# Three late loads moved behind later stores, and two rounding steps moved from the vector to the scalar engine, in the closing stage of a feed-forward kernel

## The reference, cut to what matters

```python
w = weights[conditions]                            # 128 matrices of 64x64
c = jnp.einsum('bct,bcd->bdt', x, w)               # x: 128 x 64 x 512, fp32
h = jnp.einsum('bsd,hd->bsh', c, ternarize(W1, 0.05)) + b1   # 512 -> 2048
h = jax.nn.gelu(h, approximate=False)
y = jnp.einsum('bsh,dh->bsd', h, ternarize(W2, 0.05)) + b2   # 2048 -> 512
scale = jnp.max(jnp.abs(y)) / 7.0 + 1e-08          # one scale over ALL of y
q = jnp.clip(jnp.round(y / scale), -7.0, 7.0) * scale
return x + q
```

## Time and profile before

| what | value |
|---|---|
| median of 3 runs | 1003.65 us (1003.36 to 1004.45) |
| the profiled execution, its own time | 1004.09 us |
| span of its records, first instruction to last | 1002.2 us |
| mean granted clock of the tensor engine | 0.974 |
| tensor engine busy | 925.8 us (92%) |
| vector engine, scalar engine busy | 644.5 us (64%), 547.3 us (55%) |
| main memory read, written | 60.89 MB, 16.78 MB |
| GB/s in the last four of 40 slices of 25 us | 168, 313, 385, 390 |

### The profile page before, as it was taken

The page is one execution under the profiler, slowest core; times in us unless marked ns, Lnnn a source line. Parts: engine busy times, 40 slices in busy tenths (PEclk is TensorE's granted clock), DMA queues, the critical chain, the costliest instruction groups (busy, mean ns, idle before and its releaser), DMA issues.

```text
span 1002.2 us, 14662 instructions
## 1 busy us (share of the span) xinstructions
PE 925.8 (92%) x5136; PEld 440.1 (44%) x5136; DVE 644.5 (64%) x1024; ACT 547.3 (55%) x690; POOL 144.8 (14%) x187
## 2 busy tenths in 40 slices
PE   2999999999999999999999999999999999999700
PEld 2544444444444444444444444444444444444300
DVE  7998576665656666656657666665666665633493
ACT  6886728274473827365372827446382836536190
POOL 4400030301203030200203030110303030000000
PEclk9999999999999999999999999999999999999955
DMA  9501103012212102111210301121210301204899
GB/s 341 154 2 43 43 14 82 10 42 44 50 42 51 43 10 59 32 45 42 52 42 25 69 10 42 46 48 42 52 42 10 69 23 44 84 0 168 313 385 390
DMA packets 24318, 77.86 MB, mean 78 GB/s; under 512 B 3952, under 2 KB 4080, under 8 KB 23792
## 3 DMA queue, kind: packets, MB, share of 16 engines
q1 hardware_dynamic: 20032, 73.41, 24.6%
q0 software_dynamic: 3840, 3.94, 1.4%
q10 hardware_dynamic: 432, 0.34, 0.1%
HBM read 60.89 MB, written 16.78 MB: 77 GB/s over the span
## 4 chain that ended last, share of the span: by engine, by line
PE 80%; issue 9%; DVE 5%; ACT 2%; DMA 1%; POOL 0%; SPq 0%; DVEq 0%; POOLq 0%; ACTq 0%
PE ps L433 39%; PE ps L443 37%; PE ps L413 3%; PE ps L494 3%; ACT y L706 1%; DMA y<-in_L_ffn_W 1%; DVE st L907 1%; DVE wts L866 1%; DVE wts L1046 1%; DVE wts L756 1%; DVE y L1046 0%; SPq L275 0%; DVE yc L772 0%; POOL odd L354 0%; DVE wts L911 0%
## 5 line engine op out<-in xcount | busy, mean ns | idle before, releaser
L433 PE MATMUL ps<-yc,wts 128*128 128x512 f16 x2048 | 444.9, 379 | 0.0
L443 PE MATMUL ps<-wts 128*128 128x512 f16 x1792 | 391.4, 379 | 0.0
L433 PEld LDWEIGHTS ps<-yc,wts 128*128 128x128 f16 x2048 | 200.4, 98 | 241.5 <-ACT g L610 0.4
L756 DVE SCALAR_TENSOR_TENSOR wts<-g,st,wts 128x512 f16<-128x512 f32 x256 | 186.4, 749 | 140.2 <-ACT wts L615 138.5
L610 ACT ACTIVATE g<-ps,b1t,st 128x512 f32<-128x512 f32 x256 | 197.9, 774 | 123.3 <-PE ps L433 106.7
L443 PEld LDWEIGHTS ps<-wts 128*128 128x128 f16 x1792 | 173.4, 98 | 204.8
L615 ACT ACTIVATE wts<-g,st 128x512 f16<-128x512 f32 x256 | 181.0, 713 | 0.0
L597 ACT ACTIVATE xs<-yx,st 128x2048 f16<-128x2048 f32 x28 | 56.1, 2002 | 136.8 <-DVE st L790 136.8
L365 POOL PARTITION_ALL_REDUCE st<-st x46 | 21.8, 473 | 663.3 <-DVE st L725 416.1
L348 POOL DMA_INDIRECT odd<-in_L_cond_weights,odd x112 | 110.1, 983 | 41.5 <-issue 30.0
L761 DVE SCALAR_TENSOR_TENSOR y<-ps,st,b2b 128x512 f32 (+1 forms) x56 | 41.6, 747 | 79.8 <-PE ps L443 79.7
(11 more groups left out here) (131 smaller groups left out, 366.8 us busy)
## 6 DMA issues: line engine op xcount, KB each, us to landing
yx<-in_x SPq DMA_DIRECT2D x56, 512.0 KB, 6.3
wts<-in_x SPq DMA_DIRECT2D x10, 512.0 KB, 5.4
out<-wts SPq DMA_DIRECT2D x10, 512.0 KB, 14.0
y<-in_L_ffn_W SPq DMA_DIRECT2D x8, 512.0 KB, 8.8
wts<-in_x SPq DMA_DIRECT2D x4, 1024.0 KB, 5.0
y<-in_L_ffn_W SPq DMA_DIRECT2D x4, 1024.0 KB, 20.5
y<-in_x SPq DMA_DIRECT2D x3, 1024.0 KB, 9.4
out<-wts SPq DMA_DIRECT2D x3, 1024.0 KB, 13.0
```

The lines of the kernel that those rows point to most:

```text
L433: last = nc.tensor.matmul(psH[:, j % HB, :], T1T[:, j // HC, k, j % HC * P:(j % HC + 1) * P], csp[:, a, k, :], start=(k == 0 and a == 0), ...
L443: last = nc.tensor.matmul(psY[:, r % 2, :], hsp[:, a, j, r * P:(r + 1) * P], T2T[:, j, :], start=(j == 0 and a == 0), stop=(j == HT - 1 an ...
L756: nc.vector.scalar_tensor_tensor(out=hsp[:, 1, j, :], in0=g[:, j % HB, :], scalar=s_h, in1=hsp[:, 0, j, :], op0=ALU.mult, op1=ALU.subtract ...
```

## The change

Two edits. First, `load_tail` of 13, 14 and 15 is issued behind the stores of blocks 3, 4 and 5, not 0, 1 and 2; the places that they load into stay the same. Second, `BY_VECTOR` holds piece 0 alone, so the scalar engine rounds pieces 1 and 3 too.

```diff
-        BY_VECTOR = (0, 1, 3)
+        BY_VECTOR = (0,)
...
+            WITH = 3
             stores = 0
             for i, (b, m, n) in enumerate(PIECES):
                 sp.wait_ge(o_made, i + 1)
                 for rows, source, cols in transfers(b, m, n):
                     sp.dma_start(rows_of(out_v, rows, cols), source).then_inc(o_stored, 16)
                     stores += 1
-                if i == LAST_OF[b] and b < NB - XS:
-                    load_tail(b + XS)
+                if i == LAST_OF[b] and WITH <= b < WITH + NB - XS:
+                    load_tail(b - WITH + XS)
```

## The result

| | before | after |
|---|---|---|
| median, 22 runs each | 1004.04 us (1003.36 to 1005.91) | 1005.48 us (1005.12 to 1006.7) |
| span of the profiled execution | 1002.2 us | 1003.8 us |

The ratio after to before is 1.0013, 95% interval 1.0008 to 1.0019: the changed kernel is slower by 0.8 to 1.9 us. That is clear of noise and less than the 0.2% that were called no change. On the scale of the three runs that the forecast started from (1003.65 us) the ratio gives 1004.95, inside 1003.1 to 1005.4; the bare median of the larger set, whose before is itself 0.4 higher, lies 0.1 above that range.

What follows compares the result with a forecast made beforehand. The prediction took bytes in the DMA queue, at 420 GB/s, to set the end. Its terms, -1.92, +2.3, +0.1 and 0 for roundings, gave +0.5 us; it expected 1004.1 us, range 1003.1 to 1005.4.

Steps and rivals of the forecast that it cites:

- slow stretch at 953.4 to 958 goes: Closing stage, around L13's old turn: DMA engines busy at 245 GB/s lose 1.92 us, which the change was to save.
- dry queue ahead of s2: Closing stage: after block 1's stores the DMA queue runs empty until block 2's store starts, costing 2.3 us (2.0 to 2.7).
- L13 at its new turn: Closing stage, at 962.9 to 963.6 us: L13, 3.4 to 4.1 us ahead of its turn, costs 0.1 us (0 to 1.92).
- roundings: Closing stage: moving pieces 1 and 3 to the scalar engine makes block 2 on 0.3 us later, worth 0.
- a dip of 1 us or more at L13's turn: Sign against the forecast, at about 963 us: it would mean the queue's depth isn't what hides a read.
- the read is dear wherever it stands: Rival at L13's turn: switching from stores to the first load costs 1.92 us anywhere; +2.7, 1006.4 us; chance 0.11.
- the rival beside it: Rival ahead of block 2's store: the gap is smaller, 1.4 us lost; sum -0.5, 1003.2 us; chance 0.2.
- the rival in which it never does: Rival: block 2's store finds the DMA engines still at work, so 1.92 us are saved; 1001.7 us; chance 0.04.
- their work on the same memory: Rival: ACT and DVE memory work makes 953.4 to 958 us slow, whatever is queued; -0.1 to +0.3, 1003.8 us; chance 0.1.

Runs made afterwards that it cites:

- e2: Kernel before with only the rounding edit (the vector engine rounds piece 0 alone), late loads still behind blocks 0 to 2; 1003.84 against 1003.60 us.
- e4: Changed kernel with the late loads behind the stores of blocks 6 to 8; 1005.41 us, +1.81 against the kernel before.
- f4: Changed kernel with the three late loads issued from the scalar engine, in another queue than the stores; 1003.81 us, +0.27 against the kernel before.
- e3: Changed kernel with the three late loads in reverse order, 15, 14, 13; 1005.24 us, +1.64 against the kernel before.
- f2: Changed kernel with a quarter of L13 behind block 0 and the rest behind block 3; 1004.37 us, +0.83 against the kernel before.
- g1: Kernel before with late loads issued ahead of the stores of blocks 0 to 2, in the stores' pieces; 1003.60 against 1003.58 us.
- f1: Changed kernel without the three late loads, so 3.1 MB less are moved; 996.94 us in four runs, -6.6 against the kernel before.
- f3: Changed kernel with L13 behind block 0, L14 and L15 behind blocks 6 and 7; 1004.90 us, +1.36 against the kernel before.
- g3: Changed kernel with the late loads behind blocks 1 to 3; 1003.87 us, +0.29 against the kernel before.

## Why the prediction was right in its sign and short in its size

It said +0.5 us from three terms, with the roundings at 0. They measured:

| term | forecast | measured |
|---|---|---|
| slow stretch at 953.4 to 958 goes | -1.92 | -1.92 |
| dry queue ahead of s2 (loss from 953.4 to 958) | +2.3 (2.0 to 2.7) | +1.81 |
| L13 at its new turn | +0.1 (0 to 1.92) | +1.79 |
| roundings | 0 | +0.24, within noise of 0 (e2) |

*DVE and ACT: right.* From the stage's first instruction s0a was put at +1.29 us and came at 949.55 - 948.25 = +1.30; a6 at +6.55, came at +6.51; s2's issue at +8.94, came at +8.89. DVE's wait for the scalar engine ahead of a6 was 0.64 us. The order on SP, and that DVE would not wait for the late loads, were right too.

*The dry queue: right in mechanism, 0.5 us too dear and below its bounds.* The profile has it where it was put. The price was too high because the load of the earlier trace rows was taken as the model of a store. s2 was issued at 957.14; these two windows show no byte by 958 and then nearly the full rate at once, without the crawl of a load:

```profile
957.00:958.00 1.00, 0.00 (x0) 0.00 (x0) 1.00 (x2) 1.00 (x1) 0.00 (x0) 0.50 0.00 0
958.00:959.00 1.00, 0.00 (x0) 0.00 (x0) 1.00 (x1) 1.00 (x2) 0.00 (x0) 0.50 0.97 397
```

Packets began about 0.85 us after the issue; the forecast's 2.3 us had put full rate 1.3 us after it, and these 0.4 us are nearly the whole error. The Trainium skill, DMA: Bandwidth & Descriptors, section Latency and other measured facts, has about 0.6 us to the first byte; the trace has 0.85, between that and the 1.0 that was taken. In the kernel before the load of the earlier trace rows went on like this:

```profile
905.00:906.00 1.00, 1.00 (x6) 0.49 (x5) 0.67 (x1) 0.66 (x2) 0.00 (x0) 1.00 0.77 119
906.00:907.00 1.00, 1.00 (x7) 0.45 (x5) 0.08 (x1) 1.00 (x2) 0.00 (x0) 1.00 1.05 426
```

*L13 at its new turn: wrong, and this is the step that failed.* The prediction read the earlier trace rows as: behind a short queue dear, behind a long one cheap. Two things differed between L13 and L14, the depth of the queue and which of them came first, and it chose the depth. e4, whose L13 stood 4.7 us and was dear, and f4, whose L14 stood 4.2 us and was cheap, show that depth is not it; e3 shows that the first one pays. The prediction had named a dip of 1 us or more at L13's turn as the sign that depth does not hide a read, and that sign came. The rival "the read is dear wherever it stands", given 0.11, had the mechanism, with a gap at its upper bound; the rival beside it had a gap of 1.4 us, and 1.81 lies between that and the forecast's 2.3. A sum with a dear first load and a smaller gap was never formed: the two were treated as cases that exclude each other, though they stood on different terms of one sum. With the measured terms it is -1.92 + 1.81 + 1.79 = +1.7 for the profiled pair, whose times differ by 1.6; the medians differ by 1.4.

*Luck.* The sign came from a small difference of large terms, and one term was 0.5 us too high while another was 1.7 too low. That the time on the scale of the three runs still fell inside the range is owed in part to these errors having opposite signs, and to an upper end that allowed for half of L13's price.

*The other rivals.* The queue did run dry (share 0.19 from 956 to 958 us), so the rival in which it never does fell. The slow stretch moved with the late loads while DVE and ACT worked on as before, so it is not their work on the same memory that makes it.

*What stays open* is why the first late load costs 1.5 to 1.9 us. The runs show that a quarter of a block does not pay it in full (f2), that mixing the loads in from the start gained no time (g1), and that the rate behind it is 420 GB/s and not 402, stores alone included (f1, f3). They do not show what changes in the DMA engines.

## What to carry to other kernels

Where bytes in a queue set the end, read the DMA share and the GB/s together: share low is a queue that ran dry, which the order of issues can mend; share full and GB/s low is something else, and moving the transfer moves it along. Work that can be had early (here loads whose place is free) belongs where the producer cannot yet keep the queue full; taken away from there it leaves the queue dry, and its own time is still to be spent later. And if a row allows two readings ("the first" or "the one behind a short queue"), the sum needs both, since rivals on different terms can be true at once.

## What the runs showed of the hardware that was not expected

- The first block of loads that meets a run of stores loses 1.5 to 1.9 us of DMA time with the share near 1 (1.3 up to 962 us in g3), whichever block it is (e3) and whichever of the two queues it stands in (f4). A second load that stood for a shorter time in its queue cost nothing (f4).
- Stores alone moved 400 to 403 GB/s for up to 33 us (f1), and 421 after a late load had passed (f3).
- A store to an empty queue began about 0.85 us after its issue and moved 397 GB/s in the first window after that. A load began about 1.0 us after its issue and reached full rate about 1.1 us later (119, then 426 GB/s).
- At the end of g3's profiled execution 25 GB/s were left for 2 us, the share of one DMA engine of 16. What makes such a tail is not shown.
